# A two-layer gated cross-attention kernel: the down product of the second FFN in three f16 products per chunk, its weights split by GpSimd during the attention

## The reference, cut to what matters

```python
routing_indices = jnp.argmax(router_logits, axis=-1)
for e in range(E):
    mask = (routing_indices == e)[..., None]
    xe = jnp.where(mask, hidden_states, 0.0)
    g = jnp.einsum('sbh,ih->sbi', xe, gate_w[e])
    u = jnp.einsum('sbh,ih->sbi', xe, up_w[e])
    ye = jnp.einsum('sbi,hi->sbh', jax.nn.silu(g) * u, down_w[e])
    out = out + jnp.where(mask, ye, 0.0)
...
x = x + jnp.tanh(g_ffn[1]) * L1_ffn(layernorm(x))
```

## Time and profile before

| | |
|---|---|
| median of 3 runs | 782.08 us (780.70 to 782.43) |
| the profiled execution | 779.87 us, its span 778.1 us |
| TensorE busy, share of the span | 744.4 us, 96% |
| VectorE | 609.9 us, 78% |
| ScalarE | 545.1 us, 70% |
| GpSimd | 458.2 us, 59% |
| chain that ended last, by engine | PE 67%, DVE 4%, ACT 1% |
| TensorE granted clock in the second FFN | 1.00 |

### The profile page before, as it was taken

The page is one execution under the profiler, slowest core; times in us unless marked ns, Lnnn a source line. Parts: engine busy times, 40 slices in busy tenths (PEclk is TensorE's granted clock), DMA queues, the critical chain, the costliest instruction groups (busy, mean ns, idle before and its releaser), DMA issues.

```text
span 778.1 us, 29664 instructions
## 1 busy us (share of the span) xinstructions
PE 744.4 (96%) x10488; PEld 621.2 (80%) x10489; DVE 609.9 (78%) x2369; ACT 545.1 (70%) x1101; POOL 458.2 (59%) x863
## 2 busy tenths in 40 slices
PE   5899999999899999999999999999999999999994
PEld 2688888887788868888888888888888888788883
DVE  5799999998677747787888888888889888785452
ACT  2588888886555578777777777777767777666662
POOL 5455777873022426576776767677666677427553
PEclk8699999999999999999999999999999999999998
DMA  8903999900200000000000000000000100003210
GB/s 247 304 3 123 280 269 231 230 4 3 76 1 0 1 1 3 2 8 7 0 7 7 7 7 0 7 7 7 3 4 7 32 25 0 9 8 101 70 31 12
DMA packets 56323, 41.72 MB, mean 54 GB/s; under 512 B 3929, under 2 KB 51811, under 8 KB 56016
## 3 DMA queue, kind: packets, MB, share of 16 engines
q1 hardware_dynamic: 52848, 36.53, 17.9%
q0 software_dynamic: 2272, 4.27, 1.7%
q10 hardware_dynamic: 1152, 0.27, 0.2%
HBM read 18.07 MB, written 23.44 MB: 53 GB/s over the span
## 4 chain that ended last, share of the span: by engine, by line
PE 67%; DVE 4%; issue 1%; ACT 1%; POOL 0%; DVEq 0%; POOLq 0%; ACTq 0%
PE f_bank L2069 15%; PE f_bank L56 13%; PE fold_bank L56 12%; PE fold_bank L2035 5%; PE fold_bank L959 4%; PE f_bank L965 4%; PE f_bank L1179 3%; PE fold_bank L2030 2%; PE fold_bank L1170 2%; PE fold_bank L2013 1%; PE f_bank L970 1%; PE f_bank L947 1%; PE f_bank L954 1%; DVE x_sb L1413 1%; DVE l_neg_max L1390 1%
## 5 line engine op out<-in xcount | busy, mean ns | idle before, releaser
L2069 PE MATMUL f_bank<-l_Z,l_probs 128*128 128x129 f32 x1024 | 165.4, 285 | 1.6 <-ACT l_probs L1867 0.9
L2069 PEld LDWEIGHTS f_bank<-l_Z,l_probs 128*128 128x128 f32 x1024 | 138.5, 191 | 20.9 <-DVE l_acc L1413 4.4
L1800 POOL TENSOR_TENSOR l_qk_lo<-w,l_qk_hi 128x512 f16<-128x512 f32 x128 | 144.4, 1158 | 15.4 <-ACT l_qk_hi L1882 14.7
L1413 DVE SCALAR_TENSOR_TENSOR x_sb<-f_bank,l_inv,x_sb 128x128 f32 (+1 forms) x256 | 89.8, 351 | 30.6 <-DVE l_inv L1400 5.5
L1867 ACT ACTIVATE l_probs<-fold_bank 128x512 f32<-128x512 f32 x128 | 72.7, 595 | 52.7 <-PE fold_bank L2035 52.6
L56 PE MATMUL fold_bank<-M,cT 128*128 128x512 f16 x384 | 104.1, 380 | 3.8 <-DVE l_T_lo L1384 2.9
L1857 ACT ACTIVATE w<-f_bank 128x512 f32<-128x512 f32 x124 | 74.0, 597 | 41.2 <-PE f_bank L56 39.4
L505 DVE TENSOR_REDUCE n_shared<-fold_bank 128x4 f32<-128x512 f32 x128 | 87.3, 682 | 11.2 <-PE fold_bank L742 8.6
L1872 ACT ACTIVATE l_Z<-fold_bank 128x512 f32<-128x512 f32 x124 | 74.2, 599 | 7.2 <-PE fold_bank L56 3.6
L1861 ACT ACTIVATE l_qk_hi<-w 128x512 f16<-128x512 f32 x124 | 77.4, 624 | 1.0
L1413 DVE SCALAR_TENSOR_TENSOR l_acc<-f_bank,l_inv,l_acc 128x128 f32<-128x128 f32 x224 | 76.7, 342 | 0.1
(11 more groups left out here) (311 smaller groups left out, 2313.6 us busy)
## 6 DMA issues: line engine op xcount, KB each, us to landing
expert_rows<-empty_row SPq DMA_DIRECT2D x8, 2178.0 KB, 23.8
x_sb<-expert_rows SPq DMA_DIRECT2D x39, 66.0 KB, 1.9
w<-in_L_ffn_w SPq DMA_DIRECT2D x1, 2048.0 KB, 9.3
x_sb<-in_x SPq DMA_DIRECT2D x3, 512.0 KB, 7.3
ctx_sb<-in_ctx SPq DMA_DIRECT2D x3, 512.0 KB, 8.4
w_raw<-in_L_ffn_gate_w SPq DMA_DIRECT2D x1, 1408.0 KB, 11.7
w_raw<-in_L_ffn_up_w SPq DMA_DIRECT2D x1, 1408.0 KB, 11.5
downT<-in_L_ffn_down_w SPq DMA_DIRECT2D x2, 512.0 KB, 4.3
```

What stands on the lines that cost most here:

```text
L1413: nc.vector.scalar_tensor_tensor(out=total, in0=O[:, h, 0:P], scalar=inv[:, j:j + 1], in1=total, op0=ALU.mult, op1=ALU.add).then_inc(summe ...
L1800: nc.gpsimd.tensor_tensor(qk_lo[:, w, m, Q * u:Q * u + Q].rearrange("p t n -> p (t n)"), qk[:, u, m, :], qk_hi[:, w, m, Q * u:Q * u + Q].r ...
L2069: last = nc.tensor.matmul(pv_bank[m % 2][:, h * (P + 1):(h + 1) * (P + 1)], probs[:, 2 * m + h, :], Z[:, w, 2 * m + h, :], start=True, sto ...
```

## The change

The second product is computed from a high f16 part and an f16 rest of both operands, in three f16 products per chunk of the inner width, as the first products are. Seven things go with it:

- `downT` holds the two f16 halves `down_hi` and `down_lo`. The f32 weights now land in the first part of `w2` (`down_raw`), after the first FFN's last use of it, and GpSimd splits them in twelve parts of 256 columns, one in each of the pairs 1 to 12 (`split_down`, two instructions each). Its loop over the pairs is cut in two.
- ScalarE's copy of the transposed hidden writes f16 (`hidT_hi`, the same shape).
- VectorE gets one instruction more for each tile, `hidden_lo`: the bank minus the high part.
- TensorE waits for that rest before it transposes the next hidden tile into the bank, and before the second product.
- The second products of tiles from 12 on go to two banks in turn.
- `store_all` does its small wait instruction ahead of the wait for the results.
- TensorE waits for the last split instead of the last load.

```diff
     def load(self, sp, A):
         k = self.k
+        sp.wait_ge(self.eo_done, PAIRS)
         for c, (c0, rows) in enumerate(CHUNKS):
-            sp.dma_start(k.downT[0:rows, c, :, :].rearrange("p e n -> p (e n)"), A["L1_ffn_down_w"][c0:c0 + rows, :]).then_inc(k.down_landed, 16)
+            sp.dma_start(k.down_raw[0:rows, c * E * P:(c + 1) * E * P], A["L1_ffn_down_w"][c0:c0 + rows, :]).then_inc(k.down_landed, 16)
...
+    def out_place(self, n):
+        return self.out_bank[n % 2][:, 0:P] if n >= EARLY else self.out_bank[0][:, 0:P]
...
+    def hidden_lo(self, dve, n):
+        w = n % 2
+        dve.wait_ge(self.hidT_hi_ready, n + 1)
+        self.nc.vector.tensor_tensor(self.hidT_lo[:, w, :], self.hT_bank[:, 0:self.WIDE], self.hidT_hi[:, w, :], ALU.subtract).then_inc(self.hidT_lo_ready, 1)
...
     def vector_step(self, dve, i):
         for v in range(self.U):
             if i < self.STEPS:
                 self.hidden(dve, i, v)
+            if i < self.STEPS or v == 0:
+                self.hidden_lo(dve, self.U * i + v - 1)
             if v == 1 and i + 1 < self.STEPS:
                 self.transposed_lo(dve, i + 1)
...
     def transpose_hidden(self, pe, n):
         pe.wait_ge(self.hid_ready, n + 1)
         if n:
-            pe.wait_ge(self.hidT_ready, n)
+            pe.wait_ge(self.hidT_lo_ready, n)
...
     def second_product(self, pe, n):
         k, e = self.k, self.experts["tile", n]
-        pe.wait_ge(self.hidT_ready, n + 1)
+        pe.wait_ge(self.hidT_lo_ready, n + 1)
         if n:
-            pe.wait_ge(self.result_ready, n)
+            pe.wait_ge(self.result_ready, n - 1 if n > EARLY else n)
         for c, (_, height) in enumerate(CHUNKS):
-            last = self.nc.tensor.matmul(self.out_bank[:, 0:P], self.hidT[0:height, n % 2, c * P:c * P + P],
-                                         k.downT[0:height, c, bass.ds(e, 1), :].rearrange("p a n -> p (a n)"),
-                                         start=c == 0, stop=c == len(CHUNKS) - 1)
+            down_hi, down_lo = (t[0:height, c * E * P:(c + 1) * E * P].rearrange("p (e n) -> p e n", e=E)[:, bass.ds(e, 1), :].rearrange("p a n -> p (a n)")
+                                for t in (k.down_hi, k.down_lo))
+            hid_hi, hid_lo = (t[0:height, n % 2, c * P:c * P + P] for t in (self.hidT_hi, self.hidT_lo))
+            last = both_products(self.nc, self.out_place(n), [(hid_hi, down_hi), (hid_hi, down_lo), (hid_lo, down_hi)],
+                                 start=c == 0, stop=c == len(CHUNKS) - 1)
...
+                def split_down(c):
+                    some = bass.ds(c * DOWN_STEP, DOWN_STEP)
+                    nc.gpsimd.tensor_copy(k.down_hi[:, some], k.down_raw[:, some]).then_inc(k.down_split, 1)
+                    pool.wait_ge(k.down_split, 2 * c + 1)
+                    nc.gpsimd.tensor_tensor(k.down_lo[:, some], k.down_raw[:, some], k.down_hi[:, some], ALU.subtract).then_inc(k.down_split, 1)
...
                         if not last or u == 0:
                             rests(n + 1, 1 - u)
+                    if part is not None:
+                        split_down(part)
                     if j is not None:
                         scatter(j)
...
-                with pool.Fori(1, PAIRS - 1) as i:
+                pool.wait_ge(k.down_landed, 16 * len(CHUNKS))
+                with pool.Fori(1, DOWN_PARTS + 1) as i:
+                    pair(i, i - 1, part=i - 1)
+                with pool.Fori(DOWN_PARTS + 1, PAIRS - 1) as i:
                     pair(i, i - 1)
```

More of the change, by code:

```diff
@@ L101, in prepare @@
     k.downT = sb("downT", [P, 3, E, P])
+    k.down_raw = k.w2[:, :, :, :].rearrange("p e c n -> p (e c n)")[:, 0:3 * E * P]
+    down = k.downT[:, :, :, :].rearrange("p c e n -> p (c e n)").bitcast(F16).rearrange("p (h m) -> p h m", h=2)
+    k.down_hi, k.down_lo = (down[:, h, :] for h in range(2))
+    k.down_split = ctx.enter_context(nc.semaphore("down_split"))
     k.routerT = sb("routerT", [P, E])
@@ L1013, in __init__ @@
         self.silu, self.hid = (part(2 * I1).rearrange("p (b n) -> p b n", b=2) for _ in range(2))
-        self.hidT = part(2 * self.WIDE).rearrange("p (b n) -> p b n", b=2)
+        self.hidT_hi, self.hidT_lo = (part(self.WIDE).bitcast(F16).rearrange("p (b n) -> p b n", b=2) for _ in range(2))
         self.rows_last = part(2 * ROW).rearrange("p (v n) -> p v n", v=2)
@@ L1052, in results @@
         dve.wait_ge(self.down_done, n + 1)
-        nc.vector.scalar_tensor_tensor(out=self.result[:, p, v, :], in0=self.out_bank[:, 0:P], scalar=self.k.tg[:, 3:4],
+        nc.vector.scalar_tensor_tensor(out=self.result[:, p, v, :], in0=self.out_place(n), scalar=self.k.tg[:, 3:4],
                                        in1=self.row(n), op0=ALU.mult, op1=ALU.add).then_inc(self.result_ready, 1)
@@ L1314, in second_attention @@
         HALVES = tuple(slice(HD1 * n, HD1 * n + HD1) for n in range(2))
[L1315 removed]
+        ffn.banks(tz_bank, pv_bank, (qk_bank, a_bank[0]), (a_bank[1], b_bank[0]), b_bank[1])
         def slots_of(j):
@@ L1704, in _ @@
                 sums(B - 1, 1, 7)
+                ffn.hidden_lo(dve, 0)
                 ffn.transposed_lo(dve, 1)
                 ffn.hidden(dve, 0, 2)
+                ffn.hidden_lo(dve, 1)
                 ffn.results(dve, 0, 0)
@@ L1711, in _ @@
                 ffn.hidden(dve, 1, 0)
+                ffn.hidden_lo(dve, 2)
                 dve.wait_ge(row_summed, 2 * j + 2)
@@ L1721, in _ @@
                 ffn.hidden(dve, 1, 1)
+                ffn.hidden_lo(dve, 3)
                 ffn.transposed_lo(dve, 2)
@@ L1727, in _ @@
                 ffn.hidden(dve, 1, 2)
+                ffn.hidden_lo(dve, 4)
                 for part in range(4):
@@ L1733, in _ @@
                 ffn.hidden(dve, 2, 0)
+                ffn.hidden_lo(dve, 5)
                 ffn.results(dve, 1, 1)
@@ L1737, in _ @@
                 ffn.hidden(dve, 2, 1)
+                ffn.hidden_lo(dve, 6)
                 list_left(10)
@@ L1741, in _ @@
                 ffn.hidden(dve, 2, 2)
+                ffn.hidden_lo(dve, 7)
                 ffn.results(dve, 2, 0)
                 ffn.hidden(dve, 3, 0)
+                ffn.hidden_lo(dve, 8)
                 ffn.results(dve, 2, 1)
                 ffn.hidden(dve, 3, 1)
+                ffn.hidden_lo(dve, 9)
                 ffn.results(dve, 2, 2)
                 ffn.hidden(dve, 3, 2)
+                ffn.hidden_lo(dve, 10)
                 ffn.transposed_lo(dve, 4)
```

18 lines of the change are left out of this document (9 added, 9 removed).

## The result

The changed kernel takes 783.76 us (median of 22 runs, 781.37 to 786.18) where the kernel before takes 781.53 (22 runs): 2.2 us more between the medians where 2.6 were forecast, and a ratio of 1.0031, 95% interval 1.0021 to 1.0041. The profiled execution took 782.28 us with a span of 780.6, 2.5 more than before's 778.1.

The account below looks back on a forecast made before the run. TensorE was taken to set the pace. Start +2.4, late input +0.85, steady part -1.0, end +0.2 and attention 0 gave +2.5, called 2.6; on 782.08 that is 784.7 us, range 781.6 to 787.2.

Parts of the forecast that it names:

- The second product and the bank: Second FFN, each tile: nine matmuls take 0.51 instead of 0.67; the transposed hidden's one bank allows 1.82 per tile at least.
- The register instructions: TensorE's steady part: six, then three more, behind the wait for the rest make two tiles 3.86, a step 5.93.
- rivals: TensorE's issue-bound step, 780.8, chance 0.12; only the bank's chain, 783.0, 0.18; the split showing in the attention, 788.3, 0.1.
- the rival in which only the bank's chain binds: Second FFN's steady part: a step is 5.71, -2.6 in 8.7 steps; total +0.9, 783.0; chance 0.18.
- The steady part: Second FFN from tile 12's first products to the last stretch: 8.7 steps at 5.9 instead of 6.01, -1.0 us.
- The start: Start of the second FFN: VectorE, nearly full, gets eight `hidden_lo` and tile 1's transposes come 1.1 late: +2.4.
- The late input: Tile 12: VectorE takes `hidden_lo` of tile 10 ahead of step 4's input rest, ready at 711.74 instead of 710.90: +0.85.
- The end: Last tiles: two banks remove a wait, but the rests of tiles 37 and 38 add waits: +0.2, between 0 and 0.5.
- The attention: Twelve pairs: GpSimd's copy and subtraction take 0.9 to 1.35, mostly inside its 1.22 wait for the slots: 0.
- The second result bank: Last product: two banks take away its wait for the previous tile's result, 0.64 idle; counted within the end's +0.2.

Follow-up runs that it names:

- fixed_expert: The changed kernel with the second product always taking expert 0's down weights at a fixed address, without its six register instructions per tile: ratio 1.0005.
- one_out: The changed kernel with all results of the second product in one bank, as before the change: ratio 1.0097.
- two_hT: The changed kernel with banks exchanged: from tile 12 on two in turn for the transposed hidden, one for the second product's result: ratio 1.0100.
- unwaited_rest: no_rest with a 384-column subtraction of SBUF constants at each place of `hidden_lo`, while TensorE waits for the high part alone: ratio 1.0036.
- no_rest: The changed kernel without VectorE's 39 `hidden_lo`; the third product reuses the high part and TensorE waits for ScalarE's high part alone: ratio 0.9957.
- input_first: The changed kernel with two lines exchanged at tile 12: the input's rest of step 4 ahead of `hidden_lo` of tile 10: ratio 1.0029.
- the last three kernels of the table: one_gate_fixed, one_gate_all and unwaited_rest, run when all kernels took some 7 us more: ratios 0.9986, 1.0026 and 1.0036.
- one_gate_fixed: The changed kernel with, from tile 12 on, one gate bank and two for the hidden, plus expert 0's down weights at a fixed address: ratio 0.9986.
- one_gate_all: The changed kernel with one gate bank and two for the hidden from tile 0 on, and tile 12's input rest first: ratio 1.0026.

## Why the prediction was right

It forecast +2.6 us and slower at 0.68; measured is +2.2. In absolute time it said 784.7 and 783.76 was measured; over 22 runs the kernel before is at 781.53, not at the 782.08 that it counted from. By its steps, in the profiled executions:

- **The second product and the bank.** Nine matmuls at 0.056 is right (0.51 from their first to what follows at 746.09, 0.57 at 741.90). The bank's chain was forecast at 1.82, seen at 1.80, and at 1.77 when it alone sets the pace (fixed_expert).
- **The register instructions.** The step that decided between forecast and rivals: 3.86 for two tiles was forecast; the step shown has 3.86, the mean of six 3.79, and a whole step is 5.88 against 5.9. That the one step fits to the hundredth is partly luck: from the transposes to the rest it takes 1.61 instead of 1.67, from there to the first products 1.35 (743.18 to 744.53) instead of 1.29. Taking the six instructions away gives 5.62, near the rival in which only the bank's chain binds (5.71), so that rival's mechanism was the right one to weigh, and its condition did not hold.
- **The steady part** was forecast at -1.0 and came to -0.5 from tile 11 to tile 36. The step is right: six of them, from tile 15 to tile 33, gain 0.78. But from tile 12 to tile 15 the changed kernel takes 6.39 us and the one before 6.01: that step loses 0.38 where I had it gaining 0.1. This is the term that was mis-sized. What makes it is the result bank. Two banks are used from tile 12 on, but the result of tile 12 goes to the same bank as that of tile 11, so its second product waits for VectorE's result of tile 11, which stands behind `hidden_lo` and the input's rest:

```profile
719.55 0.34 DVE L1068 SCALAR_TENSOR_TENSOR w<-f_bank,tg,x_sb 128x128 f32<-128x128 f32 x1
...
720.14 0.91 PE L58 MATMUL f_bank<-downT,w 128*128 x9 [0.19 <-DVE w L1068]
...
720.99 0.32 PE L58 MATMUL fold_bank<-w_hi,w 128*128 x1
```

  It is the only idle for a result that the view of waits lists from 714 to 765, and the step is as long as those of one_out and two_hT (6.38 to 6.51). In unwaited_rest, where no rest is waited for, it is 6.40; without VectorE's work, in no_rest, 5.68. A run in which tile 12 takes the other bank was not made.
- **The start** was forecast at +2.4: 24.16 - 21.73 = +2.43 at tile 10. The stretch that the forecast counted in grew by 2.2, between its bounds of 1.7 and 3.7. The reason given, that VectorE is full, holds for about three quarters of it (unwaited_rest, at tile 7); the waits for the rest with the register instructions behind them make what is left, which the prediction did not have in this term. Nor did it name the wait through which a full VectorE stops TensorE: three of the four idles are for the result in its one bank.
- **The late input** was forecast at +0.85: 3.34 - 2.55 = +0.79. Of it 0.53 is the order of two instructions (input_first), as forecast.
- **The end**: +0.2 forecast, +0.16 measured from the hidden transposes of tile 36 to the last result.
- **The attention**: 0 forecast. GpSimd's two instructions and the wait between them take 1.26 us where 0.9 to 1.35 was the bound, and its wait for the slots fell from 1.22 to 0.17. That VectorE's short instructions don't suffer more shows in the line of the earlier trace rows: 410 ns in the middle before, 424 now.
- **The second result bank** was right in sign and far too small. The prediction looked for its worth only where the trace of before shows an idle, at the end. It lay in the waits that `hidden_lo` would have made, 0.53 in each step, and the steps before tile 15 still pay for the one bank.

The sum in the trace is 2.43 + 0.79 - 0.52 + 0.16 = 2.86, less the 0.31 by which the second FFN began sooner in the profile of the changed kernel: 2.55 at the last result, and 2.5 in the spans. The forecast's terms add up to 2.45, 0.4 less than the 2.86. That it had rounded up to 2.6, and that the stages ahead vary by more than this between profiles, brings the totals closer than the terms are; that closeness is luck. One slip in the prediction: its forecast's own range, +1.3 to +4.4, does not follow from the terms beside it, which give +1.05 (2.55 - 1.7 + 0.2) to +4.75 (4.55 + 0.2). The measured value lies in both.

## What to carry to other kernels

A product that is made of cheaper matmuls gives TensorE time back only if the operand's rest can be had without a new wait: here 0.17 us per tile were saved, and the chain through ScalarE, VectorE and one PSUM bank, with the register instructions behind its wait, gave back all but 0.04 of it in the steady part and more than that in the rest of the stage. Count what stands in the engine's list between the end of a wait and the next matmul, address instructions included: the same nine matmuls took 0.51 to 0.57 us where the engine still had work and 0.83 behind a wait. And when a bank is scarce, ask of each product which consumer is the slower one in its queue: a second bank was worth 0.53 us per step at the result, and 0.16 at the hidden, where it had to be taken from the gate. Look also at the tile where the sharing changes: the first one can still meet the old bank.

## What the runs showed that I had not expected

- Where their code is the same, the second FFNs of different kernels' profiles agree to about a tenth of a microsecond, while the stages ahead of it vary by almost 3 us. A difference of 0.5 us that 12 runs can't tell is plain when counted from an event at the start of the stage.
- In the profiles of the last three kernels of the table, TensorE, VectorE and ScalarE stood still for some microseconds while the rows of the left tiles were being loaded; GpSimd went on issuing its stores. In the profile of unwaited_rest, ScalarE's copy for tile 7 shows 3.94 us of idle that the view puts down to no engine of this core:

```profile
710.35 0.49 ACT L1125 ACTIVATE w<-fold_bank 128x384 f16<-128x384 f32 x1 [3.94 <-remote]
```

  The transposes of tile 7, which that copy needs, had ended at 705.60. After the standstill TensorE's granted clock reads 0.50, the lower of its two levels, in 712 to 714 here, in 714 to 720 in one_gate_fixed and in 718 to 720 in one_gate_all, so that part of the 5 to 6 us is TensorE at the lower clock; it is back at 1.00 before tile 11. What held the engines is not settled.
- In the two kernels in which TensorE waits for the high part alone (no_rest, unwaited_rest), the interval that holds the input transposes is 2.19 to 2.32 us, where the changed kernel has 2.06. In the trace of no_rest ScalarE's normalised rows, which the input transposes need, end at 742.31, 0.27 ahead of them (0.60 in the changed kernel), and the second product behind them holds TensorE for 0.65 instead of 0.51, with its register instructions still running from 742.5 to 743.5. That looks like the same register instructions behind another wait, but it was not tried.
